# Two and three score banks used in turn in a six-layer attention, scan and expert kernel, with a new hand-ordered instruction order

## The reference

```python
x = x + L0_attn(layernorm(x), Wq, bq, Wk, bk, Wv, bv, Wo, bo)   # 16 heads of 32, causal softmax
x = x + L0_xattn(layernorm(x), ctx, ctx)                        # 32 query heads of 16, 8 key heads, no mask
x = x + L0_ffn(layernorm(x), w_gate, w_up, w_down)              # block-quantised silu(gate) * up, then down
x = x + L1_attn(layernorm(x), Wx, Wg, bg, Wo, A, Dp)            # selective scan: h = exp(d*A)*h + d*d
x = x + L1_xattn(layernorm(x), ctx, Wq, Wkv_expand, Wout)       # 16 heads of 32, causal softmax
x = x + L1_ffn(layernorm(x), W, gate_w, A, B)                   # top 2 of 8 low-rank experts beside a product
```

## Time and profile before

| what | value |
|---|---|
| median of 3 runs | 1620.25 us |
| span of the profiled execution | 1615.7 us |
| TensorE busy, matmuls | 1374.8 us, 12080 instructions |
| VectorE busy | 1347.9 us, 2015 instructions |
| ScalarE busy | 1038.7 us, 1884 instructions |
| GpSimd busy | 423.9 us, 488 instructions |

### The profile page before, as it was taken

One profiled execution on the slowest core, in us unless ns is written; L12 is line 12 of the kernel. 1 busy time (PEld: TensorE's weight loads), 2 busy tenths in 40 slices (PEclk: granted clock), 3 DMA queues, 4 the chain that ended last, 5 costly groups with the idle time before them and its releaser, 6 DMA issues.

```text
span 1615.7 us, 31163 instructions
## 1 busy us (share of the span) xinstructions
PE 1374.8 (85%) x12080; PEld 729.4 (45%) x12080; DVE 1347.9 (83%) x2015; ACT 1038.7 (64%) x1884; POOL 423.9 (26%) x488
## 2 busy tenths in 40 slices
PE   3778888879899999889978777879999999999986
PEld 2443445334445453444443333436455555555542
DVE  6989989979879888887898899978698888978743
ACT  3244365465673865756585768985799788989430
POOL 1432041132341522322331240241222313122210
PEclk9687979799999999999999988889999999999987
DMA  6313112200201111002130003111020211101020
GB/s 227 93 53 93 52 49 66 74 14 1 74 14 40 36 40 41 21 22 54 51 100 28 1 1 138 27 27 44 2 70 2 69 34 38 40 5 44 4 77 26
DMA packets 54194, 76.38 MB, mean 47 GB/s; under 512 B 8353, under 2 KB 23713, under 8 KB 53537
## 3 DMA queue, kind: packets, MB, share of 16 engines
q1 hardware_dynamic: 54048, 74.40, 16.3%
HBM read 39.24 MB, written 9.44 MB: 30 GB/s over the span
## 4 chain that ended last, share of the span: by engine, by line
PE 48%; DVE 29%; ACT 10%; issue 7%; POOL 3%; DMA 1%; SPq 0%; ACTq 0%; DVEq 0%; POOLq 0%
PE bank L193 17%; DVE mix_NM L1058 4%; PE bank L1158 4%; PE bank L526 3%; PE bank L534 2%; PE bank L514 2%; DVE ssm_HS L1518 2%; PE bank L971 2%; DVE ffn_m L1112 2%; PE bank L487 2%; DVE ffn_Z L1122 2%; PE bank L549 2%; PE bank L931 2%; PE bank L956 2%; DVE ffn_room L1130 1%
## 5 line engine op out<-in xcount | busy, mean ns | idle before, releaser
L1031 ACT ACTIVATE mix_P<-bank 128x512 f32<-128x512 f32 x256 | 142.2, 603 | 52.6 <-PE bank L956 50.7
L1058 DVE TENSOR_REDUCE mix_NM<-bank 128x2 f32<-128x512 f32 x256 | 164.4, 683 | 10.5 <-PE bank L931 9.8
L714 POOL TENSOR_SCALAR_AFFINE_SELECT cross_P<-cross_P 128x256 f32<-128x256 f32 x128 | 87.9, 696 | 280.3 <-ACT cross_P L628 280.0
L1276 POOL TENSOR_TENSOR ffn_room<-ffn_room 128x512 f32<-128x512 f32 x64 | 90.9, 1421 | 266.9 <-ACT ffn_room L1215 170.0
L1518 DVE TENSOR_TENSOR_SCAN ssm_HS<-ssm_DA,ssm_DD 128x1024 f32<-128x1024 f32 x64 | 150.2, 2347 | 11.4 <-ACT ssm_DD L1469 6.6
L714 POOL TENSOR_SCALAR_AFFINE_SELECT attn_P<-attn_P 128x256 f32<-128x256 f32 x128 | 86.3, 686 | 247.0 <-ACT attn_P L628 246.9
L1466 ACT ACTIVATE ssm_DA<-ssm_Z,A_T 128x255 f32<-128x255 f32 x256 | 110.8, 498 | 2.4 <-DVE ssm_HS L1518 2.1
L628 ACT ACTIVATE attn_P<-bank 128x384 f32<-128x384 f32 x128 | 63.8, 498 | 64.7 <-PE bank L515 64.2
L628 ACT ACTIVATE cross_P<-bank 128x384 f32<-128x384 f32 x128 | 62.7, 490 | 52.3 <-PE bank L515 51.7
L1524 DVE TENSOR_TENSOR ssm_HS<-ssm_HS,ssm_CS 128x1024 f32<-128x1024 f32 x64 | 80.7, 1261 | 0.9
L1441 ACT ACTIVATE ssm_Z<-bank 128x512 f32<-128x512 f32 x128 | 72.2, 598 | 13.6 <-PE bank L1354 12.9
(11 more groups left out here) (408 smaller groups left out, 4072.9 us busy)
## 6 DMA issues: line engine op xcount, KB each, us to landing
attn_stack<-attn_P SPq DMA_DIRECT2D x96, 128.0 KB, 2.4
cross_stack<-cross_P SPq DMA_DIRECT2D x96, 128.0 KB, 2.5
ffn_room<-f_gate SPq DMA_DIRECT2D x4, 1024.0 KB, 5.9
XR<-x SPq DMA_DIRECT2D x8, 512.0 KB, 6.4
ffn_room<-f_up SPq DMA_DIRECT2D x4, 1024.0 KB, 5.5
ffn_room<-f_down SPq DMA_DIRECT2D x4, 1024.0 KB, 5.5
x_mid<-XR SPq DMA_DIRECT2D x8, 512.0 KB, 3.0
XR<-x_mid SPq DMA_DIRECT2D x8, 512.0 KB, 3.8
```

The lines of the kernel that those rows point to most:

```text
L714: nc.gpsimd.affine_select(out=diagonal, in_=diagonal, compare_op=ALU.is_ge, fill=0.0, base=0, pattern=[[0, 2], [1, P]], channel_multiplier ...
L1031: nc.scalar.activation(self.p[h % 8], bank[b4[h % 2]][:, :], ACT.Exp, scale=HD2 ** -0.5).then_inc(s["p_ready"], 1)
L1058: nc.vector.tensor_reduce(self.nm[:, t, 16 * i + 2 * g:16 * i + 2 * g + 2], bank[b4[u % 3]][:, :].rearrange("p (c k) -> p c k", c=2), AX.X ...
L1276: nc.gpsimd.tensor_tensor(self.inter[q % 2][:, 512 * (g % 2):512 * (g % 2) + 512], self.sg[g % 2], self.up[g % 2], ALU.mult).then_inc(s["i ...
```

## The change

1. In both causal attentions the bank of a head's scores and of a group's output comes from a list in which banks `b[0]` and `b[1]` take turns. The sums stay in `b[2]`. ScalarE copies an output one head earlier in its order (after head 4c+7 instead of 4c+8).
2. `oc` no longer lies over `xn` but over the two halves of `xt`; the split output `ot` lies in columns 2048 to 3071 of `P`. ScalarE's normalising of X is a generator of its own, `act_norm`, with a letter of its own, and waits for the transposes of the row before. The wait for `ot_ready` moves to the first write of the next row's high half.
3. In mixing a cycle over the three banks gives two for each pair of scores, one for each half output (now 256 columns, with a copy of its own) and one for each group of transposes.
4. Mixing's final addition is four GpSimd instructions of 256 columns, each after its quarter of `xn`.
5. All five turn strings are new.

```diff
+                turns, self.scores_bank, self.out_bank = 0, [], []
+                for h in range(H1 + 3):
+                    if h < H1:
+                        self.scores_bank.append(banks[turns % 2])
+                        turns += 1
+                    if h >= 6 and h % 4 == 2:
+                        self.out_bank.append(banks[turns % 2])
+                        turns += 1
...
-                        b = self.b[0]
+                        b = self.scores_bank[h]
...
-                        o, sums = self.b[1], self.b[2]
+                        o, sums = self.out_bank[c], self.b[2]
...
-            def act(self, act, n):
+            def act_norm(self, act, n):
                 yield
                 if n:
-                    act.wait_ge(self.ot_ready, 2 * n)
+                    act.wait_ge(self.xt_ps, TT * n)
...
-                    if h >= 8 and h % 4 == 0:
+                    if h >= 7 and h % 4 == 3:
...
-                        nc.scalar.copy(self.oc[:, c, :], bank[self.b[1]][:, 0:S]).then_inc(self.o_ready, 1)
+                        nc.scalar.copy(self.oc[:, c, :], bank[self.out_bank[c]][:, 0:S]).then_inc(self.o_ready, 1)
```

Mixing:

```diff
+                in_order = itertools.cycle(banks)
+                self.scores_banks, self.out_bank, self.turned_bank = [], [], []
+                for v in range(H2 // 2 + 3):
+                    if v < H2 // 2:
+                        self.scores_banks.append((next(in_order), next(in_order)))
+                    if v >= 3 and v % 2 == 1:
+                        self.out_bank.append(next(in_order))
+                    if v >= 6 and v % 4 == 2:
+                        self.turned_bank.append(next(in_order))
...
-                        if half == 0:
-                            banks.take(b)
+                        b = self.out_bank[g]
                         pe.wait_ge(s["p_ready"], H2 * n + 4 * g + 4)
+                        banks.take(b)
...
-                        nc.scalar.copy(self.ot[:, :], bank[b4[2]][:, :]).then_inc(s["ot_ready"], 1)
+                        nc.scalar.copy(self.ot[:, g % 2 * S:(g % 2 + 1) * S], bank[self.out_bank[g]][:, 0:S]
+                                       ).then_inc(s["ot_ready"], 1)
...
-                pool.wait_ge(s["o_ready"], DC * (n + 1))
-                nc.gpsimd.tensor_tensor(x[:, :, :], x[:, :, :], self.xn[:, :, :], ALU.add).then_inc(s["x_done"], 1)
+                for c in range(DC):
+                    yield
+                    cols = slice(c * P, (c + 1) * P)
+                    pool.wait_ge(s["o_ready"], DC * n + c + 1)
+                    nc.gpsimd.tensor_tensor(x[:, :, cols], x[:, :, cols], self.xn[:, :, cols], ALU.add
+                                            ).then_inc(s["x_done"], 1)
```

The beginnings of three turn strings:

```diff
 "sp"
-ekakcekalkkaabebeeaccbebeebccbececebcbeccccbcbdaccbcdacbccdacbbcccccdccbbcdm
+aeecakkaakalkkeebbeeeccbebeccbbeececbccbccbcbcdaccdabcbcccdacbcbcccdcccbbccd
 "pe"
-aaaaaaaaaaaaaaaaaaaaaaaaaaaaaaaaaacacacaaaacaaaaaaaaaaaaaaaaaaaaaaaaaccaaaaaa
+caaccaaaaaaaaaacaaaaaaaaaaaaaaaaaaaaaaaccaaaaaaaaaaaaaaaacaaaaaaaacaaaaaacaac
 "dve"
-daggppbbgggpgppggggggggbbbbbbbbbbbbgbggggggaggggbgbbbbgggbbabbcgggdggggdggbb
+ggggggaggggpgggpbgpbdggpapaggggggggbbbbbbbbbgbbbbggggggggggggbgbbbgbgbbcbbgg
```

More of the change, by code:

```diff
@@ L1 @@
+import itertools
 from contextlib import ExitStack
@@ L83 @@
[L83 to L88 removed]
+        "caaccaaaaaaaaaacaaaaaaaaaaaaaaaaaaaaaaaccaaaaaaaaaaaaaaaacaaaaaaaacaaaaaacaacaaaaaaaaaabbaaaaaaa"
@@ L566, in pe @@
                         cols = slice(t * P, (t + 1) * P)
-                        last = product(bank[b][:, :], [(self.xt.view(lambda t_: t_[:, c, cols]),
+                        last = product(bank[b][:, :], [(self.ot.view(lambda t_: t_[:, c, cols]),
                                                         self.wo.view(lambda t_: t_[:, c, :]))],
@@ L580, in act @@
                 self.norm.act_scale(act, self.x(n), n)
+            def act(self, act, n):
                 for t in range(TT):
                     yield
+                    if n and t == 0:
+                        act.wait_ge(self.ot_ready, 2 * n)
                     act.wait_ge(self.xt_ps, TT * n + t + 1)
@@ L619, in act @@
                 nc.scalar.mul(self.nq.high[:, :], bank[self.b[2]][0:32, 0:S], 1 / RANGE).then_inc(self.nqh_ready, 1)
-                for h in range(H1 + 5):
+                for h in range(H1 + 4):
                     if h < H1:
@@ L639, in act @@
                     act.wait_ge(self.on_ready, 2 * n + half + 1)
-                    nc.scalar.copy(self.xt.high[:, two, :], self.oc[:, two, :]).then_inc(self.oh_ready, 1)
+                    nc.scalar.copy(self.ot.high[:, two, :], self.oc[:, two, :]).then_inc(self.oh_ready, 1)
             def dve(self, dve, own, n):
@@ L951, in pe @@
                             pe.wait_ge(s["v_ready"], n + 1)
-                        banks.take(b4[0], b4[1])
+                        two = self.scores_banks[v]
+                        banks.take(*two)
                         for k in range(TT):
@@ L955, in pe @@
                                 rows = slice(64 * i, 64 * i + 64)
-                                last = nc.tensor.matmul(bank[b4[i]][:, k * S:(k + 1) * S],
+                                last = nc.tensor.matmul(bank[two[i]][:, k * S:(k + 1) * S],
                                                         self.k[rows, v // 2, k * P:(k + 1) * P],
@@ L960, in pe @@
                         for i in range(2):
-                            banks.read_by(b4[i], s["p_ready"], H2 * n + 2 * v + i + 1)
+                            banks.read_by(two[i], s["p_ready"], H2 * n + 2 * v + i + 1)
                     if v >= 3 and v % 2 == 1:
@@ L1023, in act @@
                 nc.scalar.mul(self.nq.high[:, :], bank[b4[2]][0:32, 0:S], 1 / RANGE).then_inc(s["nqh_ready"], 1)
-                for h in range(H2 + 4):
+                for h in range(H2 + 5):
                     if h < H2:
```

171 lines of the change are left out of this document (87 added, 84 removed).

## The result

The kernel after takes 1650.58 us in the median (1647.94 to 1659.39, 4 runs), beside 1620.01 us (1616.87 to 1622.10, 4 runs) for the kernel before. The ratio is 1.0191, 95% interval 1.0156 to 1.0226: slower by 31 us, where I had forecast 25 us faster. The prediction was wrong, in its sign and beyond its range.

What follows compares the result with a forecast made beforehand. TensorE and VectorE were nearly full together, VectorE setting the pace from 100 to 400 us, TensorE in the long later stretches. Gains 6 + 6 + 2 + 6 + 4 + 1 = 25 us gave 1595.3 us, range 1576 to 1617.

Steps and rivals of the forecast that it cites:

- Order at the start: VectorE starts at 8 us, gaining 6 us; attention row 0's products start about 15 us later, repaid by 436.
- 6 us less idle time: VectorE between 14 and 400 us: 6 of its 36 us of idle time go; bounds 0 and 15.
- third rival: Attention row 0's delay is not repaid: +15 us, less 9 for the banks, 1626 us; chance 0.09.
- VectorE's equal work: Argument against a slower result: up to item 352, the end of feed-forward row 0, VectorE does the same items.
- TensorE's first items: Attention's transposes behind a transposition of quantised weights, waiting until about 24 us, are wanted only at 39: no cost.
- Causal banks: Scores in two banks: two thirds of waits for exponentials go; gain 2 us from 400 to 900, 6 after 1000.
- second rival: The waits on TensorE only move to the next wait; 3 us gained at the start, 1617 us; chance 0.12.
- Mixing's banks: Three banks in turn remove a quarter of the scores' waits of 19.7 to 44.0 us; gain 4 us.
- act_norm: Separate room lets the next row's scaling and transposes start without waiting for ot_ready; gain 1 us.
- Final addition: Four GpSimd parts make mixing's row ready some 1.7 us sooner, but nearly nobody waits; gain 0 us.
- fourth rival: The port lock shared with VectorE delays the 24 extra GpSimd instructions: 5 us lost, 1600 us; chance 0.05.
- The time around the span: The 4.6 us between the profiled span of 1615.7 us and the median of 1620.25, added to the forecast.

Runs made afterwards that it cites:

- M: Kernel after with the turn strings of the kernel before, except the new strings up to the end of attention row 0; 1643.59 us, ratio 1.0137.
- G: Kernel after with the turn strings of the kernel before up to the end of attention row 0, new ones after; 1646.12 us, ratio 1.0183.
- E: Kernel after with its new strings up to the end of feed-forward row 0, then those of the kernel before; 1636.67 us, ratio 1.0122.
- A: Kernel after with the turn strings of the kernel before, plus only the letters its new steps need; 1623.61 us, ratio 1.0033.
- B: Kernel after with the first half of the second weight unit's transposes moved behind the first ten product steps on TensorE; 1649.58 us, ratio 1.018.
- N: Kernel after with the strings of the kernel before up to the end of the feed-forward stage, then its new ones; 1634.82 us, ratio 1.0066.
- F: Kernel after with the strings of the kernel before through feed-forward row 0, then new, SyncE switching five items sooner; 1638.99 us, ratio 1.0112.
- H: A with ScalarE's copy of every second mixing half output one exponential earlier, as in the kernel before; 1611.61 us, ratio 0.9931.
- J: H with mixing's banks fixed as in the kernel before; 1621.78 us, ratio 1.0002.
- D: A with the banks fixed as in the kernel before, in both causal attentions and in mixing; 1629.73 us, ratio 1.0056.
- O: H with three quantising steps put at the beginning of VectorE's string; 1610.66 us, ratio 0.9936.

## Why the prediction was wrong

*Order at the start.* The step that failed is "the delay is repaid by 436 if VectorE stays full". The start of VectorE was right (7.70 us, I took 8), and L665 of row 0 too (36 and 41 us, I took 39). But VectorE did not stay full, and the delay was not repaid: TensorE, 17 us behind at 100 us, was some 16 behind at 436. VectorE had done part of its quantising early, so that less was left to put between the steps of attention's and mixing's chains: from 100 to 436 us it quantised for 118.5 us where it had for 131.5 (L788 to L818, L771 to L801 before), and its last quantising step began at 346.95 us where it had at 361.74. From 100 to 436 us it waited in the kernel after for mixing's scores, for attention's sums and for mixing's transposes,

```profile
DVE mix_NM L1085 <- PE bank L957: 15.2, 18, 3.7
DVE attn_RC L695 <- PE bank L547: 11.9, 3, 6.0
DVE mix_RS L1099 <- PE bank L1012: 11.6, 4, 5.1
```

38.7 us by these three rows, of which 14.2 lie between 350 and 400 us, when the quantising was over. In the kernel before the same three were

```profile
DVE mix_RS L1072 <- PE bank L986: 6.8, 4, 4.3
DVE attn_RC L678 <- PE bank L534: 3.8, 2, 1.9
DVE mix_NM L1058 <- PE bank L931: 3.3, 7, 1.5
```

13.9 us, 0.9 of them between 350 and 400. I had gone the other way, 6 us less idle time. What the runs show is that quantising put ahead of an attention row makes TensorE late (in M ahead of row 0, in G ahead of row 1) and that this is not repaid. That the missing filler, work without a chain to put between work with one, is the reason why it is not repaid fits the rows but was not tried by itself: in the last of these stretches, 350 to 400 us, TensorE was as busy as before (44.98 and 44.46 us), and no run changes VectorE's string alone behind the first items.

My third rival had this mechanism and this sign, and the point from which it decides (the addition of feed-forward row 0 later than 436) came as it said, at 447.67. I gave it 0.09, on "VectorE's equal work", which says nothing of when TensorE gets its work. Its price before the banks' gain was 15 us; E less A measures 0.9%, 14 us. The measured 1650.58 us still lies 25 us above its 1626, because the other losses were in no rival.

*TensorE's first items.* "It costs nothing" missed that transposes of the second unit also stand ahead of the products (18.85 us of waiting, products at 47.56, not 39). Run B shows no gain from moving them, within 0.6%.

*The later order.* I put the strings behind item 352 at nothing, without a word. They cost 0.8%, as much as the start. By what wait, and which of their letters does it, stays open: runs N and F only bound the stretches.

*Causal banks.* I had counted the new wait for L634 (L651 after) at 0.38 us, its own duration; the row of 103.61 us shows 0.85, since the exponential ahead of it counts too. Over both attentions these waits sum to 21.7 us in run H, where I had 14 at most. Nor did I count that TensorE comes sooner to the masks (6.6 us). Of the waits for exponentials more went than I took (28.8 us of 31.3, not two thirds). I took 2 and 6 us; in the old order it is 0. The second rival, that the waits only move, is right for this part alone.

*Mixing's banks.* I took 4 us. Run J, with the early copy, measures 12.6 by the spans, but 6.6 us of the waits behind them come only from half copies with a fixed bank; with the late copy of the real change (A against D) all banks in turn brought 0.2%. The 4 us lie between. The step that failed is "half a copy no longer stands before the transposes". I had compared durations of the copies (0.38 and 0.60), and not their places in ScalarE's order: the last one moved from behind exponential 11 to behind exponential 12, and costs 1.0% in the old order. The full diff showed it: `h >= 11 and h % 8 == 3` became `h >= 8 and h % 4 == 0`.

*act_norm* was taken at 1 us. It is inside the +0.4% (plus or minus 0.6) that no run takes apart, so this stays open.

*Final addition.* I took 0 and named GpSimd's queue; in the old order it gains 0.4%. Mixing's own next row waits for the addition (4.1 us in the kernel before), which I had dismissed with "nearly nobody waits behind it". The pieces are slower than a quarter of the whole: half of the 32 take 0.74 us or less, where a quarter of 2.44 is 0.61, and a few take up to 2.85, so the sum is 33.7 us in the kernel after, beside 19.5. What holds the long ones no row here names. The fourth rival's price on GpSimd was thus real in kind (14 us, of at most 25), and it did not show at the end. (It misread a row: half of the selections L714 are within 1.5% of the shortest, 409 and 403 ns, not within 1%. No sum changes by that.)

*The time around the span.* I took 4.6 us between the profiled span and the time of an execution. The executions on record have 2.1 to 3.3 us for the kernel before and about 1.7 for the kernel after: the profiled execution was 1 to 2 us faster than the median. This is 2 us of the 55 that were missed.

## What to carry to other kernels

Work that waits for nothing can fill the gaps of work that waits for a chain. Ordering it first fills the idle time at the start, but it makes the chain behind it late and leaves less to fill later gaps with, so ask of a reordering when the bounding engine gets its work, not whether another engine has the same total. When a bank is freed earlier, write out which instruction its next use waits for and what stands ahead of that one in its engine's order: here, in the old order, 28.8 us of waits turned into 28.3 us of others. And where a step is cut in two, compare the place of the last piece in the in-order queue before its duration; one exponential of 0.6 us put ahead of each of 32 copies cost about 1% in the old order.

## What the runs showed of the hardware

In the kernel after, VectorE operations on 64 elements, 0.20 us long elsewhere (as at 8.55 us in run O), took 3.53 us each at 59 and 62 us, while GpSimd filled a tile. VectorE's timeline:

```profile
58.90 3.53 DVE L793 TENSOR_SCALAR w_e<-w_max 128x64 int32<-128x64 int32 x1
...
62.47 3.53 DVE L795 TENSOR_SCALAR w_inv<-w_e 128x64 int32<-128x64 int32 x1
```

and GpSimd's:

```profile
58.88 3.51 POOL L407 MEMSET attn_stack<- 32x4096 f16 x1
...
62.44 3.51 POOL L409 MEMSET attn_stack<- 32x4096 f16 x1
```

Their ends agree to 0.1 us. Over this stretch, from 58.90 to 66.04 us, VectorE is busy some 6.7 us longer than these operations take elsewhere. In the kernel before the same two fills ran at 36.70 and 40.26 us, the second until 43.77, beside other quantising steps:

```profile
38.66 2.29 DVE L801 SCALAR_TENSOR_TENSOR ffn_room<-ffn_room,w_sc 128x2048 bf16<-128x2048 f32 x1
40.87 2.28 DVE L771 TENSOR_REDUCE w_max<-ffn_room 128x64 f32<-128x2048 f32 x1
43.19 0.63 DVE L774 TENSOR_SCALAR w_max<-w_max 128x64 f32<-128x64 f32 x1
```

The two long ones took what they take elsewhere (2.29 and 2.28 us). The small TENSOR_SCALAR, 0.20 us in run O, ended at 43.82, with the fill. In run B a long TENSOR_SCALAR (L803, 128x2048) took 2.23 us beside the same fill where it takes 1.23 elsewhere. So in these rows the kind of operation decides and not its length: TENSOR_SCALAR was held, TENSOR_REDUCE and SCALAR_TENSOR_TENSOR were not. The Trainium skill (SBUF — State Buffer, on the two separate sides) states that the two engines share a port pair as an exclusive lock that is held for a whole instruction, and that only some VectorE instructions ask for it. The held rows and the free ones both agree with that. It shows that "busy" on VectorE is in part waiting, and its 87.43 us in the first 100 us of the kernel after with it.
